# Deferring the PE half of the next block's layer norm by one output group, and evicting two PSUM banks first

## The reference

```python
xn = _layernorm(x, axis=-1)
# attention: 16 query heads, 8 key heads, D = 128
q, k, v, g = xn @ Wq, xn @ Wk, xn @ Wv, xn @ Wg
logG = cumsum(log_sigmoid(6.906768 + g))
a = where(causal, ((q . k) / sqrt(D))**2 * exp(logG[t] - logG[s]), 0)
y = (a @ v) / (sum(a) + 1e-6)
s = y @ Wc + bc
# feed-forward: 2048 -> 5632 -> 2048
hdn = silu(xn @ gate_w.T * gate_s) * (xn @ up_w.T * up_s)
out = hdn @ down_w.T * down_s
return x + s * silu(out)
```

## Time and profile before

| what | value |
|---|---|
| two timed runs | 8422.77 and 8008.34 us, median 8215.56 |
| the profiled execution | 8005.87 us |
| its span on the slowest core (core 3) | 8004.2 us; the other cores 7977.6 to 7998.6 |
| PE busy | 6775.9 us, 85% of the span |
| ACT busy | 2004.5 us, 25% |
| DVE busy | 994.7 us, 12% |
| mean granted PE clock | 0.923 to 0.925 of full speed on all cores |

### The profile page before, as it was taken

One profiled execution on the slowest core, in us unless ns is written; L12 is line 12 of the kernel. 1 busy time (PEld: TensorE's weight loads), 2 busy tenths in 40 slices (PEclk: granted clock), 3 DMA queues, 4 the chain that ended last, 5 costly groups with the idle time before them and its releaser, 6 DMA issues.

```text
span 8004.2 us, 107915 instructions; the slowest of 8 cores (7977.6 to 8004.2 us)
## 1 busy us (share of the span) xinstructions
PE 6775.9 (85%) x43624; PEld 3403.5 (43%) x43624; DVE 994.7 (12%) x2180; ACT 2004.5 (25%) x2296; POOL 557.6 (7%) x1192
## 2 busy tenths in 40 slices
PE   7999987659999897666999988777689998977777
PEld 3444433324444344433444434554234443455553
DVE  1000012220000011122000011111200000110002
ACT  2121011212210014521211011665122100146661
POOL 0000001100000000100000000000000000000000
PEclk9999998779999998888999999888799999999999
DMA  4555442253444431034444343101534444410005
GB/s 93 77 76 72 68 80 45 47 135 69 78 76 71 77 69 33 22 88 107 78 76 74 69 88 60 25 17 37 135 75 79 74 71 74 76 44 23 23 12 127
DMA packets 240203, 544.23 MB, mean 68 GB/s; under 512 B 103841, under 2 KB 112161, under 8 KB 232033
## 3 DMA queue, kind: packets, MB, share of 16 engines
q0 software_dynamic: 93392, 377.58, 28.0%
q1 hardware_dynamic: 127890, 126.18, 5.4%
q10 hardware_dynamic: 18432, 33.56, 1.6%
HBM read 864.31 MB, written 50.33 MB: 114 GB/s over the span
## 4 chain that ended last, share of the span: by engine, by line
PE 63%; ACT 12%; DMA 10%; DVE 7%; issue 4%; POOL 2%; ACTq 1%; DVEq 0%; SPq 0%; POOLq 0%
PE pball L410 30%; PE pball L464 15%; ACT a2p L719 11%; PE pball L633 3%; PE pball L752 3%; PE pball L571 3%; PE pball L546 2%; DMA out<-x 2%; DVE a2p L799 2%; DMA x<-x 2%; PE pball L862 2%; DMA ar<-wk 2%; PE pball L703 2%; POOL a2p L728 2%; DMA ar<-wq 2%
## 5 line engine op out<-in xcount | busy, mean ns | idle before, releaser
L410 PE MATMUL pball<-ar 128*128 128x512 bf16 x11264 | 2441.4, 380 | 5.2 <-DVE ar L290 5.2
L410 PEld LDWEIGHTS pball<-ar 128*128 128x128 bf16 x11264 | 1104.1, 98 | 1341.0 <-issue 18.1
L719 ACT ACTIVATE a2p<-pball,sc_tok 128x1024 bf16<-128x1024 f32 (+3 forms) x1152 | 1201.7, 1043 | 1345.7 <-PE pball L703 643.3
L464 PE MATMUL pball<-ar 128*128 128x512 bf16 x5632 | 1268.1, 386 | 89.7 <-DVE scrA L476 83.5
L752 PE MATMUL pball<-ar,a2p 128*128 128x128 bf16 x8448 | 915.3, 225 | 203.4 <-DVE ar L824 104.7
L752 PEld LDWEIGHTS pball<-ar,a2p 128*128 128x128 bf16 x8448 | 784.8, 104 | 400.0 <-issue 315.2
L703 PE MATMUL pball<-ar 128*128 128x512 bf16 x2304 | 747.3, 413 | 183.4 <-ACT a2p L719 176.9
L464 PEld LDWEIGHTS pball<-ar 128*128 128x128 bf16 x5632 | 556.8, 99 | 800.3 <-issue 165.9
L759 PE MATMUL pball<-ones_col,a2p 128*128 128x1 bf16 x8448 | 849.0, 172 | 0.0
L759 PEld LDWEIGHTS pball<-ones_col,a2p 128*128 128x128 bf16 x8448 | 736.5, 98 | 121.5 <-issue 34.9
L421 ACT ACTIVATE a2p<-pball,gsc_s 128x512 bf16<-128x512 f32 x352 | 241.9, 687 | 1866.3 <-PE pball L410 1839.6
(11 more groups left out here) (92 smaller groups left out, 2316.4 us busy)
## 6 DMA issues: line engine op xcount, KB each, us to landing
ar<-gw POOLq DMA_DIRECT2D x176, 512.0 KB, 5.2
ar<-uw POOLq DMA_DIRECT2D x176, 512.0 KB, 7.2
ar<-dw POOLq DMA_DIRECT2D x176, 512.0 KB, 5.2
ar<-wq POOLq DMA_DIRECT2D x64, 512.0 KB, 5.2
x<-x ACTq DMA_DIRECT2D x128, 256.0 KB, 3.5
ar<-wc POOLq DMA_DIRECT2D x16, 2048.0 KB, 15.9
out<-x SPq DMA_DIRECT2D x128, 256.0 KB, 3.3
x_buf<-x SPq DMA_DIRECT2D x16, 1024.0 KB, 6.5
```

The lines of the kernel that those rows point to most:

```text
L410: b.op("tensor", lambda e, half=half, cg=cg, ts=ts, bank=bank, slot=slot: e.matmul(pb[bank][:, 0:512], gu_sl(slot, half, cg), xnT_sl(cg, t ...
L464: b.op("tensor", lambda e, ic=ic, tc=tc, slot=slot: e.matmul(pb[tc][:, 0:512], hdn_sl(ic, tc * 128, 128), dn_sl(slot, ic % 4), start=(ic = ...
L719: b.op("scalar", lambda e, src=src, dst=dst, j=j, jh=jh: e.activation(dst, src, AF.Square, scale=sc_tok[:, j * 8 + jh:j * 8 + jh + 1]), ma ...
```

## The change

It has two parts. In the first, `emit_ln_chunk` is cut in two. The part up to the normalised rows is emitted where it was. The part with the 16 transposes and the two copies becomes a function, `phaseB`. Without a `deferred` list it is called at once, as at the start of the kernel. In the last stage it is kept in `lnq` and called after the next group's 8 tiles, ahead of that group's own two chunks; what is left after the fourth group is called after the loop.

In the second, the 8 banks of the last down-projection quarter are evicted in the order 6, 7, 0, 1, 2, 3, 4, 5 instead of 0 to 7.

```diff
-        def emit_ln_chunk(xsrc, xsrc_ready, tcol, bankA=6, bankB=7, dump=None):
+        def emit_ln_chunk(xsrc, xsrc_ready, tcol, bankA=6, bankB=7, dump=None,
+                          deferred=None):
...
             xn_ready = vm.n
-            for g in range(NCG):
...
-            bank_free[bankB] = (vm, vm.n)
             ln_marks.append(xn_ready)
-            return vm.n
+
+            def phaseB(xnt=xnt, tcol=tcol, bankA=bankA, bankB=bankB,
+                       xn_ready=xn_ready, par=par):
+                for g in range(NCG):
...
+                    w = [(vm, xn_ready), (s_misc, s_misc.n)]
+                    if g == 0:
+                        w += [bank_free[bankA], bank_free[bankB]]
+                    b.op("tensor", lambda e, dst=dst, g=g, xnt=xnt: e.transpose(
+                        dst, xnt[:, g * 128:(g + 1) * 128], idbf[:, :]),
+                        mark=tm, waits=w)
+                tdone = tm.n
+                ln_tp[par] = tm.n
+                for half, bank in ((0, bankA), (1, bankB)):
+                    src = pb[bank].bitcast(BF16).rearrange("p (n d) -> p n d", n=8)
+                    b.op("vector", lambda e, src=src, half=half, tcol=tcol: e.tensor_copy(
+                        xnT_3d()[:, half * 8:half * 8 + 8, tcol:tcol + 128], src),
+                        mark=vm, waits=[(tm, tdone)])
+                bank_free[bankA] = (vm, vm.n)
+                bank_free[bankB] = (vm, vm.n)
+
+            if deferred is None:
+                phaseB()
+                return vm.n
+            deferred.append(phaseB)
+            return None
...
-                        for tc in range(NTC2):
+                        ev_tcs = ([6, 7, 0, 1, 2, 3, 4, 5]
+                                  if cq == 3 and NTC2 == 8 else range(NTC2))
+                        for tc in ev_tcs:
                             b.op("vector", lambda e, tc=tc, cq=cq: e.tensor_mul(
                                 scr[:, :], pb[tc][:, 0:512], ds_b[:, cq * 512:cq * 512 + 512]),
...
+                    lnq = []
...
                         if blk + 1 < NB2:
+                            while lnq:
+                                kq, fn = lnq.pop(0)
+                                fn()
+                                if kq == NTC2 // 2 - 1 or kq == NTC2 - 1:
+                                    next_halves.append(vm.n)
                             for k in range(cb * cpc, (cb + 1) * cpc):
...
                                 b.dma("sync", sx, xb, x_d[row0n:row0n + 128, :], waits=wfree)
-                                emit_ln_chunk(xb, (sx, sx.n), k * 128, 2, 3)
-                                if k == NTC2 // 2 - 1 or k == NTC2 - 1:
-                                    next_halves.append(vm.n)
+                                dq = []
+                                emit_ln_chunk(xb, (sx, sx.n), k * 128, 2, 3, deferred=dq)
+                                lnq.append((k, dq[0]))
+                    while lnq:
+                        kq, fn = lnq.pop(0)
+                        fn()
+                        if kq == NTC2 // 2 - 1 or kq == NTC2 - 1:
+                            next_halves.append(vm.n)
```

More of the change, by code:

```diff
@@ L295, in emit_ln_chunk @@
-            ln_marks.append(xn_ready)
-            return vm.n
+            ln_marks.append(xn_ready)
+            def phaseB(xnt=xnt, tcol=tcol, bankA=bankA, bankB=bankB,
+                       xn_ready=xn_ready, par=par):
+                for g in range(NCG):
+                    bank = bankA if g < 8 else bankB
+                    dst = pb[bank].bitcast(BF16)[:, (g % 8) * 128:(g % 8) * 128 + 128]
+                    w = [(vm, xn_ready), (s_misc, s_misc.n)]
[13 more added lines that the diff above has]
+                bank_free[bankB] = (vm, vm.n)
```

## The result

The changed kernel's time is 0.989 of that of the kernel before, 95% interval 0.9848 to 0.9933; repeated in another session, where its lowest run was 7924.68 us beside 7992.16, it was 0.991, 0.9881 to 0.9938. Of 13 timed runs the median is 8476.43 us and the lowest 7919.18, of 10 runs of the kernel before 8425.5 and 8008.21. Hence the raw median lies outside my range, while 0.989 of 8008 is 7920. The gain is within the 2% that I gave as what a measurement tells from no change, but the interval leaves out 1.

The account below looks back on a forecast made before the run. It took DVE's in-order cycle in the last stage, not PE's idle, as the bound: per block 141.3 + 9.8 + 4 + 1 = 156.1 us, three blocks saving 85.2, so 8005.87 - 85.2 = 7920.7 us; range 7868 to 7960.

Parts of the forecast that it names:

- the base: Time before the change from which the saving is subtracted: profiled 8005.87 us, matching the timed run of 8008.34 us.
- DVE's cycle: Last stage, from L273 of a group's first chunk to the next group's: 61.5 us before, 47.1 us forecast.
- PE's idle: Rival: PE's 304.7 us of waits for normalised rows go, less a quarter: 229 us saved, 7777 us; chance 0.04.
- the turns of two tiles: Last stage, first to last add of a group on two residual slots: 24.4 us of each cycle.
- The collision of wc with the x rows: Last stage: next x rows are issued into the wc weight transfer and delayed, 9.8 us once per block, first cycle.
- The rival without a collision: The x rows and wc don't get in each other's way: 41 us less in all, 7879 us; chance 0.13.
- The tail and the lead: Second and third cycle: wc comes behind the x rows, meeting their tail and the first residual tiles; 2 us each.
- The sum: Per block 141.3 + 9.8 + 4 + 1 = 156.1 us; three blocks 468.3 against 553.5, 85.2 us saved.
- the two terms that I gave for it: What moves the range: tile turns at 15.0 or 19.5 us, 20 us; collisions, 41 us down and as much up.
- The eviction order: Last down-projection quarter: gate matmuls start about 8 us sooner, but the wait moves to wk: worth nothing.
- If wk were there, it would be worth up to 34.4 us: Key projection: with the wk load no longer late behind wv, evicting banks 6 and 7 first gains up to 34.4 us.

Follow-up runs that it names:

- four-slot run: Changed kernel with four residual-tile slots instead of two in the last stage; lowest run 7836.51 us.
- moving wc: Changed kernel with the wc weight load of groups 2 and 3 held back until the x rows have landed; lowest run 7913.56 us.
- wv cut: Changed kernel, two wk loads before wv, gate chain behind fourth key step, only an eighth of wv loaded; lowest run 7824.0 us, old eviction order 7857.1.
- late gates: Changed kernel, first two wk loads before wv, gate chain (tanh and DVE work) behind fourth key step; lowest run 7882.49 us, old eviction order 7875.8.

## Why the prediction was right, and where it was not

**The time: the step that failed.** It is the last one, the base. I took 8005.87 us, the profile that agrees with the lower of the two timed runs, as the kernel's time before, and called the median of 8215.56 "only their middle". Against that base the time came out within 4 us (lowest runs 7919.18 and 7924.68 for 7920.7). But over all timed runs the median before is 8425.5 and now 8476.43, 516 us above the end of my range at 7960, and only 2 of the 13 timed runs lie in the range. The medians tell nothing of the change itself, since the runs of either kernel lie more than 800 us apart. What the runs bear out is the saving, not 7920.7 us as what a run takes.

**DVE's cycle, not PE's idle, is the price.** Right. I had 47.1 us for each cycle, with 4 us added for the second and third together: 145.3 us for three. Measured on all cores: 144.5. From L274 to the next issue of x rows I had 34.4; it is 34.8, 37.5 and 34.6. The four-slot run shows that its largest term, the turns of two tiles, is real.

**The collision of wc with the x rows.** The size was right (9.8 us, measured 9.2), the place wrong. I put it "in the first cycle" and expected cycles of 56 to 58 and 47 to 50 us. But the x rows that it delays are those behind the first group, whose normalisation begins the first cycle: the delay lies ahead of the first L274, and the first cycle takes 47.7. The sum for a block is not changed by that: in the mean of all cores and blocks the way from the last stage's first matmul to the first L274 (before, L273) grew from 50.3 to 60.1 us, the three cycles fell from 183.6 to 144.5, and the rest to the next block's first matmul grew from 10.5 to 11.0. And what I had called the cost of the collision is mostly not saved by avoiding it: of the 9.2 us, 5.6 came back in the cycles. The rival without a collision (7879 us) describes a state that moving wc doesn't reach.

**The tail and the lead.** 2 us each for the second and third cycle: over the three cycles the excess on 47.1 is 3.2 us, but it lies in the second alone (+3.0).

**The sum.** 85.2 us predicted; the mean span of the repeat fell by 85.2, the last stages by 86.0. That these agree so closely is partly luck: versions with the same last stage differ by up to 15 us there. The range of 7868 to 7960 is also narrower than the two terms that I gave for it, which together reach from 7860 to 7982.

**The eviction order is worth nothing here.** Right, and for the reason given: the wait moves from L495 to wk (it grows there by 39 us and not by 31, since the gate matmuls too are done sooner). Wrong is the sentence "If wk were there, it would be worth up to 34.4 us". With the first tiles there the gain went to the tanh on ACT's queue, and with that out of the way to the third tile behind wv. Only with wv cut did it show, and then as 37.9 us: the bound left out that PE comes back from the wait at the lower clock.

## What to carry to other kernels

When work is taken from between two stretches of the engine that bounds, price the cycle of the engine that is still in the way, step by step, to where it comes round; the idle time of the first engine (here 304.7 us) says little about the gain (85). Then ask which term of that cycle is largest: two more slots of 2 KB per partition gained (77 us) nearly as much as the whole reordering. And an early start is worth something only if what stands behind it is early too: here three things stood behind it (the first wk tiles, the gates' tanh on ACT, the third wk tile behind wv), and as each was moved, the next took up the gain.

## What the runs showed of the hardware

- Small transfers are slowed beside a large one. With late gates and the new order, the second of the gates' two 16 KB transfers, which waits for the first, was issued 8.5 to 12.9 us behind it on all cores and blocks while 4096 KB of wv were under way; with 512 KB in its place it was 2.9 to 3.0 us. For the x rows (two of 1024 KB, from issue to use) it is 15.8 us beside wc and 6.6 without. The Trainium skill has a rule that could account for it (DMA: Bandwidth & Descriptors, Queues, rings and completion order): a DMA engine goes round its queues and takes a whole packet from one before it turns. The traces agree that small transfers are slowed beside large ones on other queues; how long a turn is they don't show.
- A wait of PE costs more than its length. After 8.60 us without work (kernel before, block 1, core 3) the next 32 matmuls of 128x512 took 9.54 us and not 7.07: in their first 5.0 us the granted clock was 0.50, the lower of its two levels (1.2 and 2.4 GHz), and 0.99 behind. After 21.25 us (changed kernel, block 0) the 16 matmuls of a tile took 6.01 us instead of 3.63, at a granted clock of 0.59, and 1.00 behind them.
